# The first score row as a product, and a reordered hand-over between two attention layers

## What is computed

```python
h = jnp.maximum(_layernorm(x), 0.0)
# layer 0
q = h @ Wq.T + bq;  k = h @ Wk.T + bk;  v = h @ Wv.T + bv
scores = jnp.where(adj > 0, q @ k.T / sqrt(128), neg)
x = x + jax.nn.elu(jax.nn.softmax(scores, axis=-1) @ v)
# layer 1
node = jnp.maximum(_layernorm(x), 0.0)
h = node @ W
s1 = h @ a[:128, 0];  s2 = h @ a[128:, 0]
e = jnp.where(adj > 0, leaky_relu(s1[:, None] + s2[None, :], 0.01), NEG_INF)
x = x + h + jax.nn.softmax(e, axis=1) @ node
```

## Time and profile before

| | us |
|---|---|
| time, median of 3 runs (lowest, highest) | 800.01 (799.23, 801.41) |
| the profiled execution | 797.06 |
| its span | 795.3 |
| PE busy | 725.0 (91% of the span) |
| DVE busy | 564.8 (71%) |
| ACT busy | 553.2 (70%) |
| POOL busy | 431.8 (54%) |

### The profile page before, as it was taken

How to read it: one execution, slowest core, us unless ns; L and a number is a source line. 1 busy time by engine, 2 the same in 40 slices (tenths; PEclk the granted TensorE clock), 3 DMA queues, 4 the chain that set the end, 5 groups by cost and what they waited for, 6 DMA issues and landing times. The chain is left out here.

```text
span 795.3 us, 18259 instructions
## 1 busy us (share of the span) xinstructions
PE 725.0 (91%) x6213; PEld 612.1 (77%) x6213; DVE 564.8 (71%) x1213; ACT 553.2 (70%) x1098; POOL 431.8 (54%) x337
## 2 busy tenths in 40 slices
PE   4964999999999999999999998555989999999996
PEld 2543888888888888888888887454878888888885
DVE  4847687878787878787878786158867675685572
ACT  5934668687878687878787867143996977977910
POOL 1067599999999999999999967434000000000000
PEclk9998999999999999999999999656999999999999
DMA  6059989999897989798988846813244333433100
GB/s 225 1 189 227 277 224 251 265 247 268 241 273 237 272 236 278 231 278 231 280 233 277 231 94 97 169 15 92 20 73 99 82 81 80 88 79 89 36 10 12
DMA packets 193979, 132.98 MB, mean 167 GB/s; under 512 B 174608, under 2 KB 181264, under 8 KB 185616
## 3 DMA queue, kind: packets, MB, share of 16 engines
q1 hardware_dynamic: 193200, 132.16, 62.5%
...
q0 software_dynamic: 160, 0.00, 0.0%
...
## 5 line engine op out<-in xcount | busy, mean ns | idle before, releaser
L816 DVE CUSTOM_DVE_ANT_0 scores<-ps_s,mask_both 128x1024 f32<-128x1024 f32 x128 | 155.7, 1217 | 26.9 <-POOL mask_both L620 17.5
L605 POOL TENSOR_SCALAR mask_bytes<-adj_both 128x2048 uint8<-128x2048 int32 x64 | 147.2, 2316 | 45.4 <-POOLq L80 39.7
L695 ACT ACTIVATE scores<-scores,neg_max 128x1024 f32<-128x1024 f32 x128 | 146.1, 1143 | 22.9 <-DVE neg_max L822 22.9
L835 DVE TENSOR_TENSOR low<-scores 128x1024 bf16<-128x1024 f32 x96 | 136.7, 1424 | 29.0 <-ACT scores L695 23.6
L620 POOL TENSOR_SCALAR mask_both<-mask_bytes 128x2048 bf16<-128x2048 uint8 x64 | 151.4, 2365 | 5.4 <-POOL mask_bytes L605 0.4
L1060 PE MATMUL spare<-v_parts,hiT 128*128 128x256 bf16 x768 | 141.6, 274 | 9.9 <-DMA lowT<-low 9.7
L709 ACT ACTIVATE hiT<-spare 128x512 bf16<-128x512 bf16 (+1 forms) x128 | 103.0, 805 | 59.1 <-PE spare L1041 56.4
L1061 PE MATMUL spare<-v_parts,lowT 128*128 128x128 bf16 x768 | 134.7, 220 | 0.0
L1484 PE MATMUL ps_x<-q_parts,over_k 128*128 128x258 bf16 x1024 | 118.0, 277 | 4.1 <-issue 4.1
L1014 PE MATMUL ps_s<-k_hi,q_strip 128*128 128x512 f32 x256 | 112.8, 440 | 8.4 <-DVE row_max L816 6.1
L1484 PEld LDWEIGHTS ps_x<-q_parts,over_k 128*128 128x128 fp8e4 x1024 | 100.1, 99 | 20.0 <-issue 4.1
...
## 6 DMA issues: line engine op xcount, KB each, us to landing
...
lowT<-low SPq DMA_TRANSPOSE x96, 4.7
...
mask_both<-s_row_dram SPq DMA_DIRECT2D x1, 768.0 KB, 3.9
over_k<-mask_bytes_dram SPq DMA_TRANSPOSE x16, 4.5
```

The lines of the kernel that those rows point to most:

```text
L605: nc.gpsimd.tensor_scalar(mask_bytes[b % 2][:, half(h)], adj_sb[h], 1.0, 0.0, ALU.min, ALU.max).then_inc(bytes_ready, 1)
L695: nc.scalar.activation(sc, sc, ACT.Exp, bias=neg_max[:, bn:bn + 1], accum_out=row_sum[:, bn, k:k + 1]).then_inc(exp_done, 1)
L816: nc.vector.tensor_tensor_reduce(out=scores[bn % 2][:, part(k)], in0=ps_s[k % 2][:], in1=mask[bn % 2][:, part(k)], scale=1.0, scalar=LOWES ...
L835: nc.vector.tensor_tensor(low[k][:], p, high_half(p), ALU.subtract).then_inc(low_done, 1)
```

## The change

1. **The first row as a product.** A new tile `wa_rep` holds the s1 column of `wa` in all 128 columns. PE multiplies it with the first chunk of `hT2` straight into PSUM (L1180 of the changed kernel), ACT copies it to `s1_row`. SP no longer stores and reads the row of chunk 0; two sets are left.
2. **Normalising.** POOL normalises chunks 0 to 2 in period 29, 3 to 5 in period 30, and 6 after the last period; DVE keeps chunk 7 alone. The statistics and the root are taken for strips 0 to 23 in periods 28 and 29, for 24 to 27 in period 30. PE turns chunks 0 and 1 earlier in period 31.
3. **The last strip.** DVE scales and adds the halves of strip 31 out of PSUM (`last_attention`), ACT makes the three ELU parts, DVE adds them (`last_elu`). Before, ACT, POOL, ACT and POOL did so in turn.
4. **The signs.** All first signs are ACT's, four key tiles a chunk instead of three, and each chunk's signs stand one chunk earlier in its queue. The ELU parts of strip 29 move from period 30 to period 31.
5. **PE's order.** The last chunk's turn and its `s_products` stand before three of the products with W.

The functions `variance` and `inverse_root` are cut into smaller ones with the same arithmetic (`spread_of`, `variance`, `first_guess`, `newton_step`), `early_sign` is gone, and `turn_h` waits for POOL's chunks first; the rest of the diff, cut to its core:

```diff
+        wa_rep = sb(whole, "wa_rep", [D, D], F32)
...
-        s1_in = [sem(f"s1_rows_in{i}") for i in range(3)]
+        s1_in = [sem(f"s1_rows_in{i}") for i in range(2)]
...
                     nc.vector.tensor_copy(bv_rep[:], pw[:, D:2 * D])
+                    nc.vector.tensor_scalar(wa_rep[:], ident[:], 0.0, wa[:, 0:1], ALU.mult, ALU.add)
...
-            BY_VECTOR = 2
-            S1_CHUNKS = (slice(0, 1), slice(1, 4), slice(4, NC))
+            S1_CHUNKS = (slice(1, 4), slice(4, NC))
...
-                        if last_ones and s == T - 1:
-                            normalise(BY_VECTOR + 2)
                         if has(c, b, -1):
                             add_halves(s - 1)
                         if has(c, b, 3):
                             make_bytes(*at(c, b, 3))
-                        if last_ones and s == T - 2:
+                        if last_ones and s == T - 3:
                             pool.wait_ge(bytes_ready, 2 * T)
                             pool.wait_ge(rstd_ready, 1)
-                            for n in range(BY_VECTOR, BY_VECTOR + 2):
+                            for n in range(3):
                                 normalise(n)
+                        if last_ones and s == T - 2:
+                            for n in range(3, 6):
+                                normalise(n)
                     all_periods(pool, period)
-                    normalise(5)
+                    pool.wait_ge(rstd_ready, 2)
+                    normalise(6)
                     add_elu(T - 2)
-                    normalise(6)
-                    add_halves(T - 1)
-                    split_words(0)
-                    add_elu(T - 1)
-                    for c in range(1, NC):
+                    for c in range(NC):
                         split_words(c)
                 @block.scalar
...
                             acc_copy(s - 1, b + 1)
                         copy_hiT(s, 0)
                         if not ahead:
+                            elu_exp(s - 2)
                             act.wait_ge(low_done, 3 * T - 3)
                             hT_out(0)
                         copy_hiT(s, 1)
...
                         copy_hiT(s, 3)
                         if ahead:
                             exps(s + 1, bn, 3)
-                        if before:
+                        if before and not (isinstance(c, int) and s == T - 2):
                             elu_exp(s - 1)
                     def hT_out(c):
...
                     def early_signs(c):
                         act.wait_ge(s_out, c + 1)
-                        act.wait_ge(s1_in[0], 16)
-                        for t in range(4 * c, 4 * c + 3):
+                        act.wait_ge(s1_out, 1)
+                        for t in range(4 * c, 4 * c + 4):
                             last = sign_bytes(0, s1_row, t, EARLY)
                         if c == NC - 1:
                             last.then_inc(signs_ready, 1)
                     all_periods(act, period)
                     s_out_of(0)
-                    acc_copy(T - 1, 3)
+                    act.wait_ge(s1_made, 1)
+                    nc.scalar.activation(s1_row[:, 0:512], ps_s3[1], ACT.Copy).then_inc(s1_out, 1)
+                    act.wait_ge(last_att, 1)
+                    act.wait_ge(epi_done, T - 1)
+                    nc.scalar.activation(att_neg[:], att[:], ACT.Relu, scale=-1.0).then_inc(att_cut, 1)
+                    nc.scalar.activation(att_pos[:], att[:], ACT.Relu)
+                    act.wait_ge(att_cut, T)
+                    nc.scalar.activation(att_exp[:], att_neg[:], ACT.Exp, scale=-1.0).then_inc(last_parts, 1)
                     s_out_of(1)
-                    elu_exp(T - 1)
                     hT_out(2)
                     hT_out(3)
+                    early_signs(0)
                     for c in range(2, NC - 2):
                         s_out_of(c)
-                        early_signs(c - 2)
                         if c + 2 < NC - 1:
                             hT_out(c + 2)
+                        early_signs(c - 1)
+                    hT_out(NC - 1)
                     s_out_of(NC - 2)
-                    early_signs(NC - 4)
-                    hT_out(NC - 1)
                     early_signs(NC - 3)
                     s_out_of(NC - 1)
                     early_signs(NC - 2)
...
+                    def last_attention():
+                        b = (T - 1) % 2
+                        inv = inv_by_parity[:, b:b + 1]
+                        dve.wait_ge(pv_done, 8 * T)
+                        dve.wait_ge(inv_ready, T)
+                        dve.wait_ge(halves_added, T - 1)
+                        dve.wait_ge(att_ready, T - 1)
+                        nc.vector.scalar_tensor_tensor(out=acc_sb[:, 0, :], in0=ps_a[:, 1, :], scalar=inv, in1=bv_rep[:],
+                                                       op0=ALU.mult, op1=ALU.add).then_inc(last_half, 1)
+                        dve.wait_ge(att_exp_ready, T - 1)
+                        dve.wait_ge(last_half, 1)
+                        nc.vector.scalar_tensor_tensor(out=att[:], in0=ps_a[:, 0, :], scalar=inv, in1=acc_sb[:, 0, :],
+                                                       op0=ALU.mult, op1=ALU.add).then_inc(last_att, 1)
+                    def last_elu():
+                        xs = x_sb[:, T - 1, :]
+                        dve.wait_ge(last_parts, 1)
+                        tail.do(nc.vector.scalar_tensor_tensor(out=att_exp[:], in0=att_exp[:], scalar=-1.0, in1=att_pos[:],
+                                                               op0=ALU.add, op1=ALU.add))
+                        nc.vector.tensor_tensor(xs, xs, att_exp[:], ALU.add).then_inc(last_x, 1)
+                        dve.wait_ge(last_x, 1)
+                        moments_of(T - 1)
...
-                        if not ahead:
-                            for n in range(BY_VECTOR):
-                                normalise(n)
+                        if isinstance(c, int) and s == T - 4:
+                            spread_of(FIRST)
+                        if isinstance(c, int) and s == T - 3:
+                            first_guess(FIRST)
+                            newton_step(FIRST)
                         turned_low(s, 0)
                         low_part(s, b, 1)
                         if ahead:
                             add_mask(s + 1, bn, 2)
                         turned_low(s, 1)
+                        if isinstance(c, int) and s == T - 3:
+                            newton_step(FIRST)
                         low_part(s, b, 2)
                         if ahead:
                             add_mask(s + 1, bn, 3)
...
                         if has(c, b, -3):
                             dve.wait_ge(epi_done, s - 2)
                             moments_of(s - 3)
+                        if isinstance(c, int) and s == T - 4:
+                            variance(FIRST)
+                        if isinstance(c, int) and s == T - 3:
+                            newton_step(FIRST)
+                            tail.wait()
+                            nc.vector.sem_inc(rstd_ready, 1)
                         if isinstance(c, int) and s == T - 2:
-                            variance(slice(0, 28))
-                            inverse_root(slice(0, 28))
+                            spread_of(NEXT)
+                            variance(NEXT)
+                            inverse_root(NEXT)
                             nc.vector.sem_inc(rstd_ready, 1)
...
                     moments_of(T - 3)
-                    weigh(0)
                     dve.wait_ge(epi_done, T - 1)
                     moments_of(T - 2)
                     aggregate(slice(T - 4, T - 1))
-                    weigh(1)
-                    early_sign(0)
-                    dve.wait_ge(epi_done, T)
-                    moments_of(T - 1)
+                    last_attention()
+                    weigh(0)
+                    last_elu()
                     aggregate(slice(T - 1, T))
-                    add_eps(slice(28, 32))
-                    inverse_root(slice(28, 32))
+                    add_eps(LAST)
+                    inverse_root(LAST)
                     normalise(NC - 1)
-                    early_sign(1)
-                    for c in range(2, NC - 1):
+                    for c in range(1, NC - 1):
                         weigh(c)
-                        early_sign(c)
                         if c >= 3:
...
+                        if not ahead:
+                            pe.wait_ge(masked, 4 * T)
+                            turn_h(0)
                         if before:
                             times_v(s - 1, 6)
                         if ahead:
                             make_scores(s + 1, 1 - b % 2, 2)
                         turn(s, b, 1)
+                        if not ahead:
+                            turn_h(1)
                         if before:
```

(18 more changed lines are left out.)

58 lines of the change are left out of this document (31 added, 27 removed).

## The result

The changed kernel took 790.77 us in the median of four runs (789.05 to 791.17), the kernel before on the same chip 800.71 (799.23 to 802.36): a ratio of 0.9871, with a 95% interval of 0.9846 to 0.9897. That is faster by some 10 us. The forecast was 781.2 us with a range of 776.5 to 785.0: the sign is right, but half of the gain is missing, and the time lies outside the range. The profiled execution took 789.05 us, with a span of 787.3 us, 8.0 less than before.

What follows compares the result with a forecast made beforehand. The prediction took SP's queue at the hand-over between the layers as the bound: block three 19.0 us earlier (553.95 to 534.9), plus 0.3 in block one, taken as -18.8 from 800.01, gives 781.2 us, range 776.5 to 785.0.

Steps and rivals of the forecast that it cites:

- A: Likeliest case, 60%: SP's two remaining row sets end block two; 781.2 us, between 779.5 and 783.
- The new steps of DVE in periods 28 and 29: About 17 steps of some 0.2 us, mostly in DVE's waits for ACT; 0 to 0.7 us, set at nothing.
- Step 1: Start of SP's chain: first mask transpose at 490.1, a gain of 1.2 us, taken from between 0.8 and 2.1.
- Step 2: SP's queue: eight mask transposes take 19.5 us, so the stores of chunks 1 to 3 are issued at 509.6.
- Step 3: SP's queue: three stores take 11.0 us, between 10.8 and 12.3, until their read is issued at 520.6.
- Step 4: SP's queue: stores of chunks 4 to 7, 10.96 us plus 1.2 for the read ahead; last read issued at 533.1.
- Step 5: End of block two: barrier and branch take 1.49 us after SP, so PE starts block three at 534.9.
- Do the others keep up: Block two: PE's score products, ACT, DVE and GpSimd must be done by 533.4; DVE reckoned at 527.6 to 529.1.
- Block one: `wa_rep` is one more operation at the very end of block one: +0.3 us.
- Block three: Second row set wanted about 8 us after its start, landing 525; third about 32 us after, landing about 539: in time.
- C: Rival, 20%: last stores wait for the whole 768 KB read, or GpSimd late and PE at half clock; 783.4 to 783.9.
- D: Rival, 2%: PE's clock stays at half after the hand-over, slower than before; 810 us at four strips.

Runs made afterwards that it cites:

- e5: Changed kernel with SP's wait for the second store set and its read moved from the end of block two to the start of block three: 777.62 us, 0.9769.
- e2: Changed kernel with all statistics steps of strips 0 to 23 at one place in period 29, where GpSimd is quiet: 782.10 us, 0.9828.
- e1: Kernel before with only the first row as a product, all else as it was: 781.07 us, 0.9816.
- e7: e1 with both store sets issued one behind the other and both row reads at the start of block three: 775.24 us, 0.9732.
- e8: e2 with the first set's three stores between the first four and last four mask transposes in SP's queue: 783.25 us, 0.9836.
- e11: e7 with all 32 early signs on ScalarE instead of 24: 774.62 us, 0.9712.
- e12: e2 with both row reads at the start of block three, and the second store set issued only once the first has landed: 773.99 us, 0.9710.
- e10: Changed kernel with the second set's four stores issued ahead of the first 768 KB read instead of behind it: 788.68 us, 0.9882.

## Why the prediction was wrong, point by point

- **What bounds the kernel: right.** The hand-over is where all of the difference lies. SP's queue ends block two (A), the waits for `mask_both` are gone, and a block three that begins 8.02 us earlier shortens the span by 8.0. e5 is the proof: with one wait moved off that queue, block three began 12.06 us earlier than in the changed kernel.
- **"The new steps of DVE in periods 28 and 29, about 17 of some 0.2 us ... I set them at nothing": the step that failed.** They are 18, and four of them took 5.9 us more than their own time, on the path. The 0.2 us is what such steps took in period 30 of the kernel before (0.17 to 0.21, from 478.97 to 482.47), while GpSimd was idle. The prediction had the rule in hand, that the two engines contend when VectorE reads two SBUF inputs, and even the measured pair 2.39 against 1.29, but applied it to the weighings and to GpSimd's tiles alone, and its rule leaves out the held steps that read one input. It also treated it as a slowing by a factor; it is a wait for the end of what GpSimd has running, so that a step of 0.18 us can cost as much as GpSimd's instruction, 1.9 us. With this term alone the forecast for block three would have been 540.8; the rest of the miss is in steps 2 to 4.
- **Step 1, a gain of 1.2 us, nearer to 0.8 than to 2.1: not there.** The first transpose came at 496.03. The strips ran 1.2 us ahead of those of before, which hides part of the loss in this number; e2, without the held steps and with hardly any such offset (0.05 us), shows 491.97, 0.7 us later than before. The tiles that left VectorE did give 2.0 us in period 31. But the 18 statistics steps of strips 24 to 27 in period 30 took 5.4 us (483.70 to 489.09), where those of strips 0 to 27 had taken 3.5: nine of them took 0.38 to 0.40 us each beside GpSimd's tiles. In e5 these nine took 0.16 to 0.20, and its transposes came only 0.3 us earlier against the pace of its strips, so no run shows what they cost.
- **Step 2, 19.5 us for eight transposes: 20.5.** It is 19.5 to 19.8 in the kernel before, e1 and e7, and 20.5 to 22.4 in all others (without the stretched one of e8). The reason stays open.
- **Step 3, 11.0 us for the first set: 13.8.** The range of 10.8 to 12.3 was too narrow. The same set in the same place took 9.7 in e1, 11.5 in e11, 12.0 in e12, 12.1 in e2, 12.4 in e10, 12.8 in e5 (to the wait's end; in e11 to the last landing). One look at a landing is not a price.
- **Step 4, 12.2 us for the second set: 13.4.** It took 12.9 to 14.1 in every kernel that had a read beside it. The term for the read's company was 1.2 between 0 and 3.9, and came out at 2.5 against the 10.96 of before. That it is the read that costs is not shown: e10 took it away from in front and nothing changed, and without any read e11 and e12 had landings of up to 11.4 and 10.5 us where the same four in the kernel before had 9.4 at most.
- **Step 5, 1.49 us: 1.50.**
- **Do the others keep up: yes.** ScalarE was done at 521.46 (between the 516 and 525 given), though its first early sign came at 504.32 and not near 500; the last score product at 517.4 (521.4 at half clock, 8 us less at full). VectorE ended at 531.65, 2.6 to 4.1 later than reckoned. The last strip was done at 504.7 instead of 499, in which two of the four steps, set at 0.3 us each, took 1.15 and 1.02; from the weighing of chunk 1 to the last sums it took 12.9 us instead of 17, and from there to the end 9.9 instead of 7.6. It was early enough.
- **Block one, +0.3 us:** not to be seen. The step took 0.28 us, but block two's first product came at 44.73 against 44.85 before. The 1.2 us by which the strips are ahead arise between there and strip 0's copy; no row says why. **Block three:** both rows are there when they are wanted; its first strip took 8.76 us, 1.2 less than before.
- **The sum.** 534.9 was forecast for block three. Held steps and step 1 add 5.9, the transposes 1.0, the first set 2.8, the second 1.2, the rest 0.1: 11.0, which makes 545.9. Of the rivals C came nearest in kind (longer stores, late GpSimd), but it charged GpSimd's lateness to itself, where it fell on VectorE. In its own text the prediction also has slips that change nothing: the lower clock stands in three slices and not in four, the lower end of A adds up to 779.1 and not 779.5, and the 791 in D comes from no sum.
